# Normalising the tokens of a latent stage on ScalarE by scale and shift instead of on VectorE by mean and scale

## The chip, the core and the metric

The kernel runs on one core of one Trainium2 chip. The metric is the device time of one execution in microseconds, the median of three timed runs. Beside it stands one profiled execution, whose trace is read here. A core has five engines that run their own queues in order and wait for each other by semaphores: TensorE (PE; its weight loads are PEld), VectorE (DVE), ScalarE (ACT), GpSimd (POOL), and SyncE (SP), which here only issues DMAs.

## What is computed

Two layers of attention and experts over 4096 tokens of 256 numbers. The change touches the first step alone, the normalisation of the first layer's input, whose result goes to the attention and to the experts. The reference, cut to that:

```python
def _layernorm(x, axis=-1, eps=1e-05):
    m = jnp.mean(x, axis=axis, keepdims=True)
    v = jnp.var(x, axis=axis, keepdims=True)
    return (x - m) / jnp.sqrt(v + eps)

x = L0_attn_x                       # (2, 2048, 256)
xn = _layernorm(x, axis=-1)
x = x + _L0_attn_ref(xn, ...) + _L0_ffn_ref(xn, ...)

# first lines of _L0_attn_ref(xn, ...)
q = (x @ Wqa @ Wqb).reshape(b, s, H, D)
kv = (x @ Wkva @ Wkvb).reshape(b, s, KVH, D, 2)
k, v = (kv[..., 0], kv[..., 1])
q = _rope(q)
k = _rope(k)
```

## The kernel before

The program is a row of stages with a barrier between each two: `latents`, `attention`, `layer1_weights`, `experts`, `mixing`, `layer1`, `finish`. The change is in `latents`, which makes the normalised tokens, the queries, keys and values of the first layer and the router's logits.

`latents` cuts the 4096 tokens into 8 chunks (c = 0 to 7) of 512, each of four tiles (t) of 128 tokens. A chunk goes through these steps:

- VectorE: `statistics` (`bn_stats` over each tile, L397), `variances` (`bn_aggr`, then `var_eps`, the variance plus epsilon, four numbers per partition, L402 to L406). ScalarE: `std`, a square root (L278). VectorE: `normalise` (reciprocal `rstd`, L410, then (x - mean) * rstd for each of four tiles of 128x256, L415) into `xn`.
- TensorE: `turn` transposes the chunk (L347) into `pT`; ScalarE copies it to `xnT` (L283). TensorE: `combined` makes the latents (L355), ScalarE copies them to `comb` (L287).
- TensorE: three `pair`s (k = 0, 1, 2) of products (L363): queries in two halves, keys in the third. VectorE: `products` multiplies each pair by cosine and sine (`by_cos` L424, `by_sin` L425).
- Each of the three is then split into three bf16 parts. GpSimd: `turned` adds the two products to `rot` (L252). ScalarE: `high` (L292). GpSimd: `left` subtracts to `rest` (L258). ScalarE: `mid` (L296). VectorE: `low` (L429). SP stores the parts.
- TensorE and VectorE: values and logits (L369, L372, L435, L437).

Nothing but the order in which the code is written sets the order on an engine. A chunk c on VectorE does products 0, `statistics(c+2)`, products 1, products 2, `variances(c+2)`, low 0, `values`, `normalise(c+2)`, low 1, low 2. On ScalarE: the two copies to `xnT` of chunk c+1, high 0, mid 0, high 1, the copy to `comb` of chunk c+1, high 2, `std_of(c+2)`, mid 1, mid 2. On GpSimd: rot 0, rest 0, rot 1, rot 2, rest 1, rest 2. On TensorE: pair 0, `turn(c+1)`, pair 1, pair 2, `combined(c+1)`, values and logits. The first two chunks are normalised ahead of the loop. Chunks 6 and 7 have nothing left to normalise.

Of the kernel before, what the change touches and what calls it, by code (L numbers as in the profile page):

```python
# [24 lines left out]
ALU = mybir.AluOpType  # L25
ACT = mybir.ActivationFunctionType
# [75 lines left out]
def latents(nc, d, s):  # L102

    with ExitStack() as ctx:  # L104
        def sb(name, shape, dt=F32):
            return ctx.enter_context(nc.sbuf_tensor(name, shape, dt))
# [21 lines left out]
        mean_var = sb("mean_var", [P, TPC, 2])  # L128
        var_eps = sb("var_eps", [P, TPC])
        std = sb("std", [P, TPC])  # L130
        rstd = sb("rstd", [P, TPC])
        xn = [sb(f"xn{u}", [P, TPC, E]) for u in range(2)]
        xnT = [sb(f"xnT{u}", [P, EC, CH]) for u in range(2)]
        comb = [sb(f"comb{u}", [COMB, CH]) for u in range(2)]
# [140 lines left out]
        def _(act):  # L275
            def std_of(c):
                act.wait_ge(var_ready, 5 * c + 5)
                act.activation(std[:], var_eps[:], ACT.Sqrt).then_inc(std_ready, 1)  # L278

            def xnT_copy(c):  # L280
                act.wait_ge(xnT_made, c + 1)
                for k in range(EC):
                    act.copy(xnT[c % 2][:, k], pT[:, k]).then_inc(xnT_ready, 1)  # L283
# [14 lines left out]
            def chunk(c):  # L298
                if c + 1 < NCH:
                    xnT_copy(c + 1)  # L300
                high(c, 0)
                mid(c, 0)
                high(c, 1)
                if c + 1 < NCH:
                    comb_copy(c + 1)
                high(c, 2)
                if c + 2 < NCH:
                    std_of(c + 2)
                mid(c, 1)
                mid(c, 2)  # L310

            for dst, src in (
# [5 lines left out]
            ):  # L318
                act.dma_start(dst, src).then_inc(weights_in, 16)
            std_of(0)  # L320
            act.wait_ge(weights_in, 16 * 5)

            q_pair = wqb[0:QL].rearrange("k (n two) -> k n two", two=2)
# [3 lines left out]
            for dst, src in (  # L327
# [3 lines left out]
            ):  # L331
                act.copy(dst, src).then_inc(swapped, 1)
            std_of(1)
            xnT_copy(0)
            comb_copy(0)
            for c in range(NCH):
# [56 lines left out]
        def _(dve):  # L393
# [4 lines left out]

            def variances(c):
                dve.wait_ge(stats_ready, 4 * c + 4)  # L400
                wait(dve, xn_ready, 4 * c)
                dve.memset(carrier[:], 0.0)  # L402
                for t in range(TPC):
                    dve.bn_aggr(mean_var[:, t], stats[:, t]).then_inc(var_ready, 1)
                dve.wait_ge(var_ready, 5 * c + 4)
                dve.tensor_scalar(var_eps[:], mean_var[:, :, 1], LN_EPS, None, ALU.add).then_inc(var_ready, 1)  # L406

            def normalise(c):
                dve.wait_ge(std_ready, c + 1)
                dve.reciprocal(rstd[:], std[:]).then_inc(rstd_ready, 1)  # L410
                dve.wait_ge(rstd_ready, c + 1)
                wait(dve, xn_out[c % 2], 16 * (c // 2))
                wait(dve, xnT_made, c - 1)
                for t in range(TPC):
                    dve.tensor_scalar(xn[c % 2][:, t], x[c % 2][:, t], mean_var[:, t, 0:1], rstd[:, t:t + 1],  # L415
                                      ALU.subtract, ALU.mult).then_inc(xn_ready, 1)

            def products(c, k):
                n = PAIRS * c + k
# [19 lines left out]
            def chunk(c):  # L439
                ahead = c + 2 < NCH  # L440
                products(c, 0)
                if ahead:
                    statistics(c + 2)
                products(c, 1)
                products(c, 2)
                if ahead:
                    variances(c + 2)
                low(c, 0)
                values(c)
                if ahead:  # L450
                    normalise(c + 2)
                low(c, 1)
                low(c, 2)

# [6 lines left out]
            for c in range(2):  # L461
                statistics(c)
                variances(c)
                normalise(c)
            dve.wait_ge(tables_in, 32)
            for c in range(NCH):
                chunk(c)
# [2060 lines left out]
```

## Time and profile before

| | us |
|---|---|
| median of three runs | 2151.51 |
| lowest, highest | 2150.54, 2153.01 |
| the profiled execution, its own time | 2145.62 |
| span of its trace | 2143.9 |

Over the span TensorE is busy 92%, VectorE 72%, ScalarE 48%, GpSimd 23%. `latents` ends at 120.4 us, and 62.6 of GpSimd's 492.4 us lie in it. Times in the rows below count from the span's start. A timeline row gives the start, the busy time, the engine, line, operation, what it writes and reads with its shape, and how many instructions it merges ("x2"); in brackets stands how long the engine had been idle and who released it.

### The profile page before, as it was taken

To read this page: it belongs to the slowest core of one execution; us is meant where nothing else is said; L and a number is where in the kernel's file an instruction comes from. 1 tells how busy PE (TensorE), PEld (TensorE's weight loads), DVE (VectorE), ACT (ScalarE), POOL (GpSimd) and SP (SyncE) were. 2 spreads that over 40 slices of the span, in tenths; PEclk is the share of its full clock that TensorE was granted. 3 is DMA by queue.
4 is the path that set the end of the run, shared out by engine and by line. 5 is a ranking of instruction groups with operands and counts; after the bars stand their busy time and mean duration, and the time that the engine had idled before them with its cause. 6 is when DMAs were issued, how large, how long until landed. Compare 5 with 4: busy or idle time off the path is not lost. (4 is left out here: it accounts for less than half of the span.)

```text
span 2143.9 us, 35036 instructions
## 1 busy us (share of the span) xinstructions
PE 1973.5 (92%) x11857; PEld 1190.7 (56%) x11874; DVE 1549.3 (72%) x3492; ACT 1026.7 (48%) x2224; POOL 492.4 (23%) x908
## 2 busy tenths in 40 slices
PE   7869999999999999999579999996878999999998
PEld 3313333333333333332279999995656777777777
DVE  6879888888888888885145333324669998899893
ACT  3406677777777777777444444543331122221112
POOL 4621133322222222222223333335600000000000
PEclk9958999999999999999889999998889999999998
DMA  5572011111111111100332322214510000000005
GB/s 189 186 230 78 29 46 58 56 43 41 41 43 43 42 43 41 43 21 11 92 114 88 110 97 88 89 45 148 167 55 2 18 20 20 20 20 20 3 11 169
DMA packets 119460, 143.69 MB, mean 67 GB/s; under 512 B 12152, under 2 KB 107008, under 8 KB 118912
## 3 DMA queue, kind: packets, MB, share of 16 engines
q1 hardware_dynamic: 89392, 99.48, 14.5%
q0 software_dynamic: 7680, 20.98, 3.1%
q10 hardware_dynamic: 22224, 21.16, 2.9%
q8 instruction: 88, 1.44, 0.3%
q14 instruction: 76, 0.62, 0.1%
HBM read 85.10 MB, written 56.10 MB: 66 GB/s over the span
## 5 line engine op out<-in xcount | busy, mean ns | idle before, releaser
L715 ACT ACTIVATE at_wt<-at_B 128x512 f32<-128x512 f32 (+3 forms) x1280 | 606.9, 538 | 243.0 <-PE at_B L764 237.1
L965 DVE TENSOR_REDUCE at_piece_max<-at_A 128x1 f32<-128x512 f32 x768 | 487.1, 683 | 53.0 <-PE at_A L745 51.1
L782 PE MATMUL at_O<-at_wt,at_v 128*32 128x512 f32 (+3 forms) x2560 | 312.3, 540 | 0.0
L669 POOL TENSOR_SCALAR_AFFINE_SELECT at_wt<-at_wt 128x128 f32<-128x128 f32 x512 | 147.8, 294 | 658.9 <-ACT at_wt L715 650.2
L745 PE MATMUL at_A<-at_k,at_q 96*128 96x512 bf16 (+3 forms) x800 | 275.2, 353 | 8.5 <-DVE at_piece_max L962 2.4
L962 DVE CUSTOM_DVE_ANT_0 at_junk<-at_A,at_hide 128x128 bf16<-128x128 f32 (+3 forms) x512 | 230.3, 487 | 65.9 <-PE at_A L745 62.9
L764 PE MATMUL at_B<-at_q,at_k 99*128 99x512 bf16 (+3 forms) x800 | 272.7, 348 | 2.0 <-ACT at_wt L715 2.0
L1425 PE MATMUL ex_H<-ex_xT,ex_w_in 128*128 128x256 f32 x1920 | 247.4, 285 | 3.2 <-DVE ex_xT L1532 3.2
L1425 PEld LDWEIGHTS ex_H<-ex_xT,ex_w_in 128*128 128x128 f32 x1920 | 236.5, 192 | 3.6 <-DVE ex_w_out L1537 3.6
L1546 DVE TENSOR_TENSOR ex_h<-ex_act_a,ex_H 128x256 f32<-128x256 f32 x160 | 66.8, 417 | 212.4 <-ACT ex_act_a L1474 212.3
L745 PEld LDWEIGHTS at_A<-at_k,at_q 96*128 96x128 bf16 x800 | 77.7, 97 | 214.7 <-DVE at_piece_max L965 108.9
L745 PE MATMUL at_A<-s_k,s_q 96*128 96x512 bf16 (+2 forms) x480 | 175.8, 384 | 20.9 <-PEq L104 9.6
L2111 ACT ACTIVATE l_act_g<-l_G 128x512 f32<-128x512 f32 x80 | 47.9, 599 | 305.2 <-PE l_G L2025 249.9
L1467 POOL TENSOR_TENSOR ex_hT<-ex_h,ex_hT 128x256 fp32r<-128x256 f32 x160 | 123.2, 774 | 265.5 <-ACT ex_hT L1478 265.5
L764 PE MATMUL at_B<-s_q,s_k 99*128 99x512 bf16 x480 | 160.2, 352 | 4.7 <-ACT at_wt L715 4.1
L2046 PE MATMUL l_D<-s_down,l_h 128*128 128x256 f32 x640 | 153.6, 383 | 3.5 <-DVE l_h L2192 3.5
L2046 PEld LDWEIGHTS l_D<-s_down,l_h 128*128 128x128 f32 x640 | 120.1, 191 | 35.0 <-issue 13.5
L2166 DVE TENSOR_TENSOR l_order<-l_order 128x1024 f32<-128x1024 f32 x112 | 136.9, 1222 | 1.9
L2020 PE MATMUL l_G<-l_xp,s_gate_up 128*128 128x512 f32 x480 | 137.2, 420 | 0.0
L2164 DVE TENSOR_TENSOR l_order<-l_order 128x1024 f32<-128x1024 f32 x112 | 136.5, 1219 | 0.0
L745 PEld LDWEIGHTS at_A<-s_k,s_q 96*128 96x128 bf16 x480 | 47.0, 99 | 151.1 <-DVE at_piece_max L965 76.8
L2030 PE MATMUL l_U<-l_xp,s_gate_up 128*128 128x512 f32 x480 | 130.2, 406 | 0.0
(262 smaller groups left out, 2633.3 us busy)
## 6 DMA issues: line engine op xcount, KB each, us to landing
buf<-s_down ACTq DMA_DIRECT2D x10, 1024.0 KB, 10.5
ex_x<-buf SPq DMA_DIRECT2D x40, 256.0 KB, 2.7
expert_out<-ex_y ACTq DMA_DIRECT2D x40, 256.0 KB, 2.2
ex_raw_in<-in_W_in SPq DMA_DIRECT2D x8, 1024.0 KB, 4.9
q_parts<-parts SPq DMA_DIRECT2D x16, 384.0 KB, 3.4
s_down<-in_x SPq DMA_DIRECT2D x8, 512.0 KB, 4.8
xn<-xn SPq DMA_DIRECT2D x8, 512.0 KB, 5.6
at_v<-v SPq DMA_DIRECT2D x16, 256.0 KB, 3.4
```

Source lines behind the costliest of these rows:

```text
L669: pool.affine_select(block_, block_, [[1, P]], ALU.is_ge, 0.0, base=0, channel_multiplier=-1).then_inc(hidden, 1)
L715: act.activation(wt[(HP * p + h) % NE_][:, q0:CH], pB_of(p, h, u)[:, q0:CH], ACT.Exp, scale=D ** -0.5).then_inc(wt_ready, 1)
L745: pe.matmul(pA[slot % NA][:, 0:w], q[n % 3][0:STACK, h, i * P:(i + 1) * P], k[n % 3][0:STACK, k0:k0 + w], start=True, stop=True).then_inc( ...
L764: pe.matmul(pB_of(p, h, u)[:, q0:CH], k[n % 3][:, kt * P:(kt + 1) * P], q[n % 3][:, h, j * CH + q0:(j + 1) * CH], start=True, stop=True).t ...
L782: pe.matmul(pO[j % 2][rows, q0:CH], vs[n % 3][:, kt // TPC, kt % TPC, :], wt[(HP * p + h) % NE_][:, q0:CH], start=kt < 2 and not late, sto ...
L962: ins = dve.tensor_tensor_reduce(junk[(HP * i + h) % 4][:, 0:w], pA[slot % NA][:, 0:w], hide[:, CH - w:CH], 1.0, NEG, ALU.add, ALU.max, ac ...
L965: ins = dve.tensor_reduce(top, pA[slot % NA][:, 0:w], AX.X, ALU.max)
L1425: ins = pe.matmul(pH[f][:, a, :], w_in[w][wq][:, k, cols], xT[i][xq][:, k, :], start=(n == 0), stop=(n == len(terms) - 1))
L2020: ins = pe.matmul(pG[i % 2][:], s[f"gate_up{b}"][:, e, k, :], xp[c % 2][:, a, k, :], start=(a, b, k) == steps[0], stop=(e >= NX and (a, b, ...
L2046: ins = pe.matmul(pD[t // 2][:, t % 2, :], h[i % 2][:, t * P:(t + 1) * P], s["down"][:, ORDER[i], :], start=False, stop=(i == MLPS - 1 and ...
L2164: dve.tensor_tensor(dv[:, :, half:size], high, low_m, ALU.min).then_inc(sort_step, 1)
L2166: dve.tensor_tensor(dv[:, :, 0:half], low, high_m, ALU.max).then_inc(sort_step, 1)
```

## The change

The four normalisations of a chunk move from VectorE to ScalarE. There xn = rstd * x + shift is one activation per tile, with scale and bias read per partition. VectorE makes rstd and shift = -mean * rstd (`scales`, one reciprocal and one `scalar_tensor_tensor` on four numbers per partition) in two buffers each. `variances(c+2)` goes ahead of products 2, and `scales(c+2)` stands right behind products 2. On ScalarE `std_of(c+2)` goes ahead of the copy to `comb`, and the four activations (`normal(c+2)`) stand between mid 1 and mid 2. For the first two chunks, `normal(0)` stands behind the first `std`, and `normal(1)` behind the second, ahead of the first copy to `xnT`.

```diff
--- before.py
+++ after.py
@@ -128,7 +128,8 @@
         mean_var = sb("mean_var", [P, TPC, 2])
         var_eps = sb("var_eps", [P, TPC])
         std = sb("std", [P, TPC])
-        rstd = sb("rstd", [P, TPC])
+        rstd = [sb(f"rstd{u}", [P, TPC]) for u in range(2)]
+        shift = [sb(f"shift{u}", [P, TPC]) for u in range(2)]
         xn = [sb(f"xn{u}", [P, TPC, E]) for u in range(2)]
         xnT = [sb(f"xnT{u}", [P, EC, CH]) for u in range(2)]
         comb = [sb(f"comb{u}", [COMB, CH]) for u in range(2)]
@@ -277,6 +278,14 @@
                 act.wait_ge(var_ready, 5 * c + 5)
                 act.activation(std[:], var_eps[:], ACT.Sqrt).then_inc(std_ready, 1)
 
+            def normal(c):
+                act.wait_ge(rstd_ready, 2 * c + 2)
+                wait(act, xn_out[c % 2], 16 * (c // 2))
+                wait(act, xnT_made, c - 1)
+                for t in range(TPC):
+                    act.activation(xn[c % 2][:, t], x[c % 2][:, t], ACT.Identity, bias=shift[c % 2][:, t:t + 1],
+                                   scale=rstd[c % 2][:, t:t + 1]).then_inc(xn_ready, 1)
+
             def xnT_copy(c):
                 act.wait_ge(xnT_made, c + 1)
                 for k in range(EC):
@@ -301,12 +310,14 @@
                 high(c, 0)
                 mid(c, 0)
                 high(c, 1)
+                if c + 2 < NCH:
+                    std_of(c + 2)
                 if c + 1 < NCH:
                     comb_copy(c + 1)
                 high(c, 2)
+                mid(c, 1)
                 if c + 2 < NCH:
-                    std_of(c + 2)
-                mid(c, 1)
+                    normal(c + 2)
                 mid(c, 2)
 
             for dst, src in (
@@ -318,6 +329,7 @@
             ):
                 act.dma_start(dst, src).then_inc(weights_in, 16)
             std_of(0)
+            normal(0)
             act.wait_ge(weights_in, 16 * 5)
 
             q_pair = wqb[0:QL].rearrange("k (n two) -> k n two", two=2)
@@ -331,6 +343,7 @@
             ):
                 act.copy(dst, src).then_inc(swapped, 1)
             std_of(1)
+            normal(1)
             xnT_copy(0)
             comb_copy(0)
             for c in range(NCH):
@@ -398,22 +411,20 @@
 
             def variances(c):
                 dve.wait_ge(stats_ready, 4 * c + 4)
-                wait(dve, xn_ready, 4 * c)
+                wait(dve, rstd_ready, 2 * c)
                 dve.memset(carrier[:], 0.0)
                 for t in range(TPC):
                     dve.bn_aggr(mean_var[:, t], stats[:, t]).then_inc(var_ready, 1)
                 dve.wait_ge(var_ready, 5 * c + 4)
                 dve.tensor_scalar(var_eps[:], mean_var[:, :, 1], LN_EPS, None, ALU.add).then_inc(var_ready, 1)
 
-            def normalise(c):
+            def scales(c):
                 dve.wait_ge(std_ready, c + 1)
-                dve.reciprocal(rstd[:], std[:]).then_inc(rstd_ready, 1)
-                dve.wait_ge(rstd_ready, c + 1)
-                wait(dve, xn_out[c % 2], 16 * (c // 2))
-                wait(dve, xnT_made, c - 1)
-                for t in range(TPC):
-                    dve.tensor_scalar(xn[c % 2][:, t], x[c % 2][:, t], mean_var[:, t, 0:1], rstd[:, t:t + 1],
-                                      ALU.subtract, ALU.mult).then_inc(xn_ready, 1)
+                wait(dve, xn_ready, 4 * (c - 1))
+                dve.reciprocal(rstd[c % 2][:], std[:]).then_inc(rstd_ready, 1)
+                dve.wait_ge(rstd_ready, 2 * c + 1)
+                dve.scalar_tensor_tensor(shift[c % 2][:], mean_var[:, :, 0], -1.0, rstd[c % 2][:],
+                                         ALU.mult, ALU.mult).then_inc(rstd_ready, 1)
 
             def products(c, k):
                 n = PAIRS * c + k
@@ -442,13 +453,13 @@
                 if ahead:
                     statistics(c + 2)
                 products(c, 1)
+                if ahead:
+                    variances(c + 2)
                 products(c, 2)
                 if ahead:
-                    variances(c + 2)
+                    scales(c + 2)
                 low(c, 0)
                 values(c)
-                if ahead:
-                    normalise(c + 2)
                 low(c, 1)
                 low(c, 2)
 
@@ -461,7 +472,7 @@
             for c in range(2):
                 statistics(c)
                 variances(c)
-                normalise(c)
+                scales(c)
             dve.wait_ge(tables_in, 32)
             for c in range(NCH):
                 chunk(c)
```

One chunk on ScalarE, from its copies to `xnT` to the next ones, before:

```order
L283 COPY xnT<-pT 128x512 x2
L292 CAST parts<-rot 128x512
L296 CAST parts<-rest 128x512
L292 CAST parts<-rot 128x512
L287 COPY comb<-pC 104x512
L292 CAST parts<-rot 64x512
L278 ACTIVATE std<-var_eps 128x4
L296 CAST parts<-rest 128x512
L296 CAST parts<-rest 64x512
L283 COPY xnT<-pT 128x512 x2
```

and changed:

```order
L292 COPY xnT<-pT 128x512 x2
L301 CAST parts<-rot 128x512
L305 CAST parts<-rest 128x512
L301 CAST parts<-rot 128x512
L279 ACTIVATE std<-var_eps 128x4
L296 COPY comb<-pC 104x512
L301 CAST parts<-rot 64x512
L305 CAST parts<-rest 128x512
L286 ACTIVATE xn<-s_down,shift,rstd 128x256 x4
L305 CAST parts<-rest 64x512
```

The square root stands two places earlier, and four activations stand between the last two `mid` (parts<-rest). No table load stands in either.

The same chunk on VectorE, from its second products to its first `low` and the values, before:

```order
L424 TENSOR_TENSOR by_cos<-pR,cos 128x512 [waits lat_pair_made]
L425 TENSOR_TENSOR by_sin<-pR,sin 128x512
L424 TENSOR_TENSOR by_cos<-pR,cos 64x512 [waits lat_pair_made]
L425 TENSOR_TENSOR by_sin<-pR,sin 64x512
L402 MEMSET carrier 128x1 [waits lat_xn_ready,lat_stats_ready]
L404 BN_AGGR mean_var<-stats 128x2 x4
L406 TENSOR_SCALAR var_eps<-mean_var 128x4 [waits lat_var_ready]
L429 TENSOR_TENSOR parts<-rest,parts 128x512 [waits lat_mid_ready]
```

and changed:

```order
L435 TENSOR_TENSOR by_cos<-pR,cos 128x512 [waits lat_pair_made]
L436 TENSOR_TENSOR by_sin<-pR,sin 128x512
L415 MEMSET carrier 128x1 [waits lat_rstd_ready,lat_stats_ready]
L417 BN_AGGR mean_var<-stats 128x2 x4
L419 TENSOR_SCALAR var_eps<-mean_var 128x4 [waits lat_var_ready]
L435 TENSOR_TENSOR by_cos<-pR,cos 64x512 [waits lat_pair_made]
L436 TENSOR_TENSOR by_sin<-pR,sin 64x512
L424 RECIPROCAL rstd<-std 128x4 [waits lat_xn_ready,lat_std_ready]
L426 SCALAR_TENSOR_TENSOR shift<-mean_var,rstd 128x4 [waits lat_rstd_ready]
L440 TENSOR_TENSOR parts<-rest,parts 128x512 [waits lat_mid_ready]
```

The aggregates and `var_eps` stand ahead of the third products instead of behind them, and reciprocal and shift ahead of the first `low` instead of behind the values.

Ahead of the loop, the changed ScalarE, from the copies of weights to the first copy of turned tokens:

```order
L344 COPY wv<-wkvb 32x64
L279 ACTIVATE std<-var_eps 128x4 [waits lat_var_ready]
L286 ACTIVATE xn<-s_down,shift,rstd 128x256 [waits lat_rstd_ready]
L286 ACTIVATE xn<-s_down,shift,rstd 128x256 x3
L292 COPY xnT<-pT 128x512 [waits lat_xnT_made]
```

Before, the copy to `xnT` stood right behind the square root.

## Rows read from the trace of the kernel before

**Rows 1.** Windows, first stage: length; busy us of PE, PEld, DVE, ACT, POOL; clock; DMA

```profile
0.00:120.40 120.40, 85.83 (x288) 40.38 (x288) 87.38 (x212) 45.93 (x87) 62.64 (x61) 0.95 0.55 182
```

**Rows 2.** Windows, each from one chunk's first `by_cos` to the next one's; columns as above

```profile
21.58:33.94 12.36, 10.77 (x45) 5.73 (x44) 11.42 (x26) 5.46 (x10) 7.65 (x6) 1.00 0.18 54
33.94:45.88 11.94, 9.74 (x38) 4.62 (x37) 10.48 (x28) 5.38 (x10) 7.61 (x6) 1.00 0.60 194
45.88:58.51 12.63, 11.30 (x38) 4.99 (x37) 11.14 (x27) 5.47 (x10) 7.75 (x6) 0.86 0.53 181
...
70.46:83.33 12.87, 11.35 (x40) 5.45 (x39) 11.34 (x28) 5.47 (x10) 7.62 (x6) 0.89 0.56 184
83.33:95.27 11.94, 9.73 (x38) 4.62 (x37) 10.48 (x27) 5.37 (x10) 7.62 (x6) 1.00 0.55 188
95.27:106.20 10.93, 10.38 (x33) 4.31 (x31) 7.05 (x12) 5.27 (x9) 7.56 (x6) 1.00 0.55 191
```

**Rows 3.** Timeline of chunk 5

```profile
86.43 0.67 DVE L425 TENSOR_TENSOR by_sin<-pR,sin 128x512 f32<-128x512 f32 x1
86.67 1.16 POOL L258 TENSOR_TENSOR rest<-rot,parts 128x512 f32<-128x512 f32 x1 [0.73 <-ACT parts L292]
...
87.79 3.01 POOL L252 TENSOR_TENSOR rot<-by_cos,by_sin 128x512 f32<-128x512 f32 x2
...
88.63 0.46 DVE L406 TENSOR_SCALAR var_eps<-mean_var 128x4 f32<-128x4 f32 x1
...
90.76 2.26 POOL L258 TENSOR_TENSOR rest<-rot,parts 128x512 f32<-128x512 f32 x2
...
91.81 1.37 DVE L415 TENSOR_SCALAR xn<-s_down,mean_var,rstd 128x256 f32<-128x256 f32 x1
91.95 0.62 ACT L296 CAST parts<-rest 128x512 bf16<-128x512 f32 x1 [0.39 <-POOL rest L258]
93.06 0.62 ACT L296 CAST parts<-rest 64x512 bf16<-64x512 f32 x1 [0.49 <-POOL rest L258]
94.07 1.28 DVE L429 TENSOR_TENSOR parts<-rest,parts 128x512 bf16<-128x512 f32 x2
...
94.20 1.09 PE L347 MATMUL pT<-s_ident,xn 128*128 128x128 f32 x8 [1.97 <-DVE xn L415]
```

**Rows 4.** Timeline of chunk 0 (first row) and chunk 4

```profile
27.95 2.15 DVE L406 TENSOR_SCALAR var_eps<-mean_var 128x4 f32<-128x4 f32 x1
...
75.29 1.26 POOL L252 TENSOR_TENSOR rot<-by_cos,by_sin 128x512 f32<-128x512 f32 x1 [0.34 <-DVE by_sin L425]
...
75.79 0.68 DVE L424 TENSOR_TENSOR by_cos<-pR,cos 64x512 f32<-64x512 f32 x1 [0.57 <-PE pR L363]
...
77.00 0.17 DVE L404 BATCH_NORM_AGGREGATE mean_var<-stats 128x2 f32<-128x6 f32 x1
...
77.40 1.07 DVE L406 TENSOR_SCALAR var_eps<-mean_var 128x4 f32<-128x4 f32 x1
```

**Rows 5.** Timeline of the start, ahead of the loop

```profile
10.69 0.52 ACT L332 COPY wqb_swap<-wqb 64x128 f32<-64x128 f32 x2 [2.88 <-DMA wkvb<-in_Wkvb]
...
11.93 0.20 ACT L278 ACTIVATE std<-var_eps 128x4 f32<-128x4 f32 x1
12.04 1.05 ACT L283 COPY xnT<-pT 128x512 f32<-128x512 f32 x2
...
12.38 1.38 DVE L415 TENSOR_SCALAR xn<-s_down,mean_var,rstd 128x256 f32<-128x256 f32 x4
...
21.58 0.69 DVE L424 TENSOR_TENSOR by_cos<-pR,cos 128x512 f32<-128x512 f32 x1 [7.82 <-PE pR L363]
```

**Rows 6.** ScalarE in later stages: group (count, busy us, mean ns, idle), then timeline rows

```profile
L1732 ACT ACTIVATE mx_xn<-mx_x,mx_shift,mx_rstd 128x256 f32<-128x256 f32 x32 | 17.5, 593 | 8.0 <-DVE mx_shift L1792 8.0
...
1560.65 1.09 ACT L1732 ACTIVATE mx_xn<-mx_x,mx_shift,mx_rstd 128x256 f32<-128x256 f32 x2 [0.50 <-DVE mx_shift L1792]
...
1595.96 1.71 ACT L2127 ACTIVATE s_down<-s_down,l_mean 128x256 f32<-128x256 f32 x4 [4.61 <-DVE l_mean L2258]
```

## What I expected

> **What bounds the kernel now.** I read the windows by stage first. The first stage (`latents`) takes 120.4 us of the 2143.9 us span [rows 1], and the change touches nothing else. What follows starts behind a barrier and keeps its instructions, so a microsecond won or lost in `latents` is a microsecond of the kernel. Then I cut the stage at the start of each chunk's first product (`by_cos`). That gives the period of each chunk: 12.36, 11.94, 12.63, 11.95, 12.87, 11.94 us for chunks 0 to 5, and 10.93 for chunk 6 [rows 2]. Chunks 0 to 5 each normalise chunk c+2; chunk 6 doesn't. So at most the normalising costs 73.69 - 6 x 10.93 = 8.1 us in all. Of the six, chunks 1, 3 and 5 repeat each other to 0.01 us; chunks 0, 2 and 4 are longer.
>
> Last I read the timeline of chunk 5 backwards from 95.27, where the next chunk's first product starts [rows 3]. VectorE has no gap there: two `low` (1.28 us from 94.07), before them the four normalisations from 91.81. The first of them alone lasts 1.37 us, until just behind GpSimd's last `rest` (90.76 + 2.26 = 93.02); where GpSimd is idle, all four take 1.38 [rows 5]. ScalarE had its last `mid` done at 93.06 + 0.62 = 93.68, so the second `low`, which starts about 0.6 us after the first, at 94.67, waits for VectorE alone. TensorE waits for the same four: its turning of the tokens starts at 94.20 after 1.97 us idle. So two chains run side by side between GpSimd and the next product: the four normalisations on VectorE, done at 94.1, and mid(c,2) on ScalarE, done at 93.7 with its low a microsecond later. Under both lies GpSimd's own loop (rot, rest, rot, rot, rest, rest), the 10.93 us of chunk 6.
>
> **The change, part by part.**
>
> *Price of the moved step.* The same operation with scale and bias read per partition, 128x256, stands in the mixing stage: 593 ns each, and two in a row take 1.09 us, so the next starts 0.50 us after the one before [rows 6]. Four take 3 x 0.50 + 0.59 = 2.09 us, and the next ScalarE instruction starts 2.0 us after the first. With a scale alone four took 1.71 us [rows 6]; that is my lower bound. On VectorE they were 1.38 (alone) to 2.34 us. A page speaks against such a move: the Trainium skill, "ScalarE: Activation LUTs", section "Rules for kernel authors", says to keep multiplying and adding on VectorE. It gives no sum here, and the rows (2.09 against 1.38) lean its way. No table load is added: the sequence of ScalarE shows none.
>
> *Where it stands.* ScalarE does mid(c,1), then the four, then mid(c,2). In chunk 5, mid(c,1) runs 91.95 to 92.57 and rest(c,2) is ready at 93.02 [rows 3]. Only 0.5 us of the 2.0 lies in a gap of ScalarE. mid(c,2) would start at 92.5 + 2.0 = 94.5 instead of 93.06, end at 95.15, and low(c,2) start at 95.2 instead of 94.67: **+0.5 us**. The next product follows low(c,2) as before. low(c,1), now free of the four, is done before and helps nobody. TensorE gets its tokens at about 94.6 instead of 94.15 and stays as late as the product is. The break-even of the four is 1.5 us.
>
> *What is pushed ahead of the third products.* `variances` now stands between products(c,1) and products(c,2). In chunk 5 the second products end at 86.43 + 0.67 = 87.10. The aggregates take 0.40 us (77.00 to 77.40 in [rows 4]), so `var_eps` is issued at 87.5, inside GpSimd's rest(c,0), which runs to 87.83. The rows show that `var_eps`, four numbers per partition, waits for GpSimd: 88.63 + 0.46 = 89.09, just behind the end of rot(c,1) [rows 3]. In chunk 0 it lasted 2.15 us, through the end of one GpSimd instruction and a whole further one [rows 4]. So it ends at about 87.9, the third products at 89.2, and rot(c,2) starts at 89.25 instead of 89.05: +0.2. Before, low(c,0) stepped between rot(c,1) and rot(c,2), and the two took 3.01 us instead of 2 x 1.26 [rows 3]. Now it comes later, behind `scales`, and steps in behind rot(c,2) or behind rest(c,1). In the first case rest(c,1) ends some 0.35 us later than before, in the second at about the same time. Of these two cases I take **+0.1**, between 0 and 0.35. A page bears on them: the Trainium skill, "SBUF — State Buffer", section "Who interferes with whom", says that a VectorE operation with two SBUF inputs and a GpSimd one that reads SBUF exclude each other for the length of an instruction. By that rule `shift`, which has two, waits for rot(c,2) and lets rest(c,1) go ahead of low(c,0), the second case, and the sum would be 0.3 us less; no row here shows a `shift` beside GpSimd.
>
> With the +0.5 above that makes +0.6 us a chunk for chunks 1, 3 and 5, bounds +0.2 (four at 1.71 us) and +0.9.
>
> *Chunks 0, 2 and 4.* There TensorE is late with the second pair. In chunk 4 its granted clock averages 0.89 [rows 2]. rot(c,1) starts at 75.29, right behind products(c,1), and runs to 76.55 [rows 4]. `var_eps` comes 0.4 us behind the products, at 75.6, so inside rot(c,1), and waits for its end. Before, products(c,2) started at 75.79; now they start at 76.65: **+0.85** for rot(c,2), rest(c,1) and mid(c,1). Walked on: products to 77.95, rot(c,2) 78.03 to 79.29, a short `shift`, rest(c,1) to 80.6, mid(c,1) to 81.2, the four to 83.2, mid(c,2) to 83.75, low(c,2) to 84.5, next product at 84.4 instead of 83.33: +1.1. I walked chunks 0 and 2 the same way and got +1.2 and +1.15. If low(c,0) steps in ahead of rest(c,1) it is +1.45. I take **+1.15** each, bounds +0.7 and +1.5.
>
> *Hidden.* `std` now goes ahead of the copy of comb: that delays the copy by 0.2 us, and TensorE's next products, which need comb, stand just ahead of its 1.97 us of waiting [rows 3]. The reciprocal and `shift` end by 90.8 in chunk 5 even if `shift` waits for rot(c,2); the four start at 92.5. The order of SP's queue is unchanged; low(c,0) and its store come 1.6 us later, and nobody reads that store for a chunk and more.
>
> *Start.* This part is bare. xnT_copy(0) stood right behind std(1), at 12.04 [rows 5]. Now normal(1) stands between. It needs the reciprocal and `shift` behind std(1). In the mixing stage, where reciprocal and shift stand between them in the same way, ScalarE sits idle 0.50 us [rows 6]; std(1) ends at 12.13, so the four start at 12.6. 12.6 + 2.0 = 14.6 for xnT_copy(0): **+2.55 us**. VectorE's first product waited 7.82 us for TensorE at 21.58 [rows 5], and TensorE for this copy, so nothing covers it. normal(0) starts half a microsecond behind the first `std`, at 8.3, and ends near 10.4, ahead of the weights, which ScalarE takes up at 10.69 [rows 5]; it costs nothing. Bounds: +2.2 (four at 1.71) and +3.4, if TensorE's rise to the higher of its clocks falls later in its own work too (0.85, as chunks with time at the lower clock are 0.7 to 0.9 us longer [rows 2]).
>
> *Sum.* 2.55 + 3 x 0.6 + 3 x 1.15 = 7.8 us. The profiled execution took 2145.62 us; the three timed ones have the median 2151.51, 5.9 more, and I add the difference to that: **2159.3 us** (+0.36%). By the bounds: 2.2 + 0.6 + 2.1 = 4.9 and 3.4 + 2.7 + 4.5 = 10.6.
>
> **The rivals.**
>
> *A, no change.* The loop is more elastic than my walk: GpSimd's three last instructions are no longer disturbed by VectorE, `var_eps` slips between two of them in all chunks, and the four cost about 1.7 us. Then a chunk pays 0.2 us: 2.2 + 6 x 0.2 = +3.4, 2154.9 us. For it: GpSimd's pairs take 3.01 where two undisturbed ones take 2 x 1.26 [rows 3, 4]. Against: `var_eps` was held in each chunk whose rows stand here (0.46, 1.07 and 2.15 us, where four numbers alone want under 0.2).
>
> *B, faster.* The four vanish beside ScalarE's waits, and each chunk falls to GpSimd's 10.93 us. That is -8.1 + 2.55 = -5.5 us, 2146.0. Place: between mid(c,1) and mid(c,2). It decides from a length of the four of 0.5 us, the gap there; the rows give 2.0. For it speaks only that ScalarE is busy 5.4 of 12 us [rows 2].
>
> *C, slower still.* `var_eps` loses to rot(c,1) in chunks 1, 3 and 5 too, as it lost one more GpSimd instruction in chunk 0 [rows 4]. Each then pays 1.2 us more: +3.6, in all +11.4, 2162.9. On the same side: TensorE, idle longer in each chunk, is granted the lower of its two clocks (1.2 and 2.4 GHz) more often. It had it, after its wait for the tokens, in chunks 2 and 4, and those were 0.7 and 0.9 us longer than chunk 5 [rows 2].
>
> Beyond the stage one thing is not fixed: attention begins at the lower clock, and the end of that stretch may move by a microsecond either way.
>
> **How the numbers follow.** Forecast (+4.3 to +10 us) 0.62, A 0.19, B 0.04, C 0.15. A measurement of this kernel tells 0.2%, 4.3 us, from no change. A lies within it, B beyond it on the fast side. So faster 0.04, same 0.19, slower 0.77. The range leaves out B, the half of A near zero and the tail of C: 2154.0 to 2164.0.
>
> **What would show it.** The four activations at 0.50 us spacing, mid(c,2) starting right behind them, with low(c,2) waiting for it on VectorE; chunk periods near 12.5 and 13.5 to 14, chunk 6 still 10.9; `var_eps` ending just behind a GpSimd instruction; first product at 24.1. I am wrong if the four are much shorter, if mid(c,2) still waits for rest(c,2), or if the period of chunks 1, 3, 5 stays at 11.9. Then the start alone is left and the kernel is unchanged within the measurement.

## The result and the profile after

The changed kernel takes 2162.06 us in the median of six runs (2157.49 to 2162.6), against 2150.43 us for the kernel before in six runs (2146.95 to 2153.01). The ratio is 1.005, with a 95% interval of 1.0038 to 1.0063: 0.5% slower. Measured once more, in experiment e10, the ratio is 1.006 (1.0039 to 1.0082). I had forecast 2159.3 us and a range of 2154 to 2164.

The profiled execution took 2161.9 us, its span is 2160.2. Attention's first matmul starts at 129.91 us, where it started at 120.44 before. So 9.5 us of the difference between the two traces lie in `latents`. The rest, 6.8 us, lies in stages whose instructions are the same in both: from attention's first matmul to the next stage's 942.6 us against 939.3, and 516.5 against 513.3 in `layer1`. The two later traces, e10 of the changed kernel and e11 of the kernel before, show nearly the same again: 941.9 against 939.7, and 516.4 against 513.4. The longer `layer1` is not the change's, since two versions of the kernel before, e5 and e8, have it too (516.4 and 516.5). What lengthens attention by 2 to 3 us stays open.

One timed run of e3 took 2801.02 us at a mean granted clock of 0.647, and e3's ratio is without it.

The stage, cut at each chunk's first `by_cos` as in [rows 2] (length; busy us of PE, PEld, DVE, ACT, POOL with counts; granted clock; DMA share; GB/s):

```profile
23.93:36.14 12.21, 10.74 (x45) 5.70 (x44) 10.29 (x24) 7.34 (x14) 7.67 (x6) 1.00 0.19 54
36.14:48.07 11.93, 9.72 (x37) 4.61 (x37) 10.07 (x24) 7.23 (x14) 7.65 (x6) 1.00 0.60 193
48.07:61.84 13.77, 11.32 (x37) 5.02 (x37) 10.35 (x25) 7.34 (x14) 7.70 (x6) 0.88 0.52 169
61.84:75.71 13.87, 11.31 (x37) 5.01 (x37) 10.34 (x25) 7.34 (x14) 7.69 (x6) 0.87 0.48 166
75.71:89.75 14.04, 11.35 (x37) 5.05 (x36) 10.34 (x24) 7.34 (x14) 7.69 (x6) 0.86 0.50 168
89.75:103.79 14.04, 11.35 (x36) 5.43 (x36) 10.35 (x24) 7.34 (x14) 7.70 (x6) 0.86 0.52 168
103.79:115.61 11.82, 11.82 (x36) 5.41 (x34) 6.55 (x12) 5.37 (x9) 7.55 (x6) 0.90 0.52 171
```

Chunks 0 and 1 are as long as before (12.21 and 11.93 against 12.36 and 11.94). Chunks 2 to 5 are longer by 1.14, 1.92, 1.17 and 2.10 us, and chunk 6 by 0.89. From chunk 2 on TensorE has the lower of its two clocks for a part of every chunk (a mean granted clock of 0.86 to 0.90). Before, that was so in chunks 2 and 4 (0.86 and 0.89), and for a moment in chunk 3 (0.98). ScalarE is busy 7.3 us of a chunk, where it was 5.4.

The timeline of chunk 4 (start, busy time, what, idle before and releaser), which answers to [rows 4] and to the end of [rows 3]:

```profile
79.16 0.69 DVE L435 TENSOR_TENSOR by_cos<-pR,cos 128x512 f32<-128x512 f32 x1 [0.86 <-PE pR L376]
...
80.52 1.27 POOL L253 TENSOR_TENSOR rot<-by_cos,by_sin 128x512 f32<-128x512 f32 x1 [0.32 <-DVE by_sin L436]
80.78 1.04 DVE L419 TENSOR_SCALAR var_eps<-mean_var 128x4 f32<-128x4 f32 x1
...
83.08 1.26 POOL L253 TENSOR_TENSOR rot<-by_cos,by_sin 64x512 f32<-64x512 f32 x1 [1.29 <-DVE by_sin L436]
83.12 1.24 DVE L426 SCALAR_TENSOR_TENSOR shift<-mean_var,rstd 128x4 f32<-128x4 f32 x1
...
84.28 0.68 DVE L440 TENSOR_TENSOR parts<-rest,parts 128x512 bf16<-128x512 f32 x1
84.30 2.78 POOL L259 TENSOR_TENSOR rest<-rot,parts 128x512 f32<-128x512 f32 x2
...
86.53 2.07 ACT L286 ACTIVATE xn<-s_down,shift,rstd 128x256 f32<-128x256 f32 x4
...
88.51 0.60 ACT L305 CAST parts<-rest 64x512 bf16<-64x512 f32 x1
...
88.65 1.51 PE L360 MATMUL pT<-s_ident,xn 128*128 128x128 f32 x8 [2.69 <-ACT xn L286]
...
89.14 0.68 DVE L440 TENSOR_TENSOR parts<-rest,parts 64x512 bf16<-64x512 f32 x1 [1.50 <-ACT parts L305]
```

Read it from the top. TensorE is late with the second pair. rot(c,1) starts behind it, and `var_eps`, issued 0.26 us later, is held until rot(c,1) ends. The third products wait for `var_eps`, so GpSimd sits idle 1.29 us ahead of rot(c,2). Then the four activations take 2.07 us, mid(c,2) starts right behind them, and low(c,2) waits for mid(c,2). TensorE waits 2.69 us for the tokens, where no such wait was above 1.97 us in the kernel before (the one of chunk 5 stands in [rows 3]). The lower clock begins during the eight transposes behind the wait: they take 1.51 us here, 1.09 at the higher clock.

`shift` is issued 0.04 us behind the start of rot(c,2) and held until that ends, 1.24 us. Then low(c,0) starts 0.02 us ahead of rest(c,1), and the two `rest` take 2.78 us, where they took 2.26 in [rows 3]. So it is in chunks 2 to 5. In chunks 0 and 1 `shift` is held by rest(c,1) as well, for 1.70 and 1.45 us, and low(c,0) comes behind rest(c,1).

The start, which answers to [rows 5]:

```profile
11.77 0.21 ACT L279 ACTIVATE std<-var_eps 128x4 f32<-128x4 f32 x1
...
12.42 2.07 ACT L286 ACTIVATE xn<-s_down,shift,rstd 128x256 f32<-128x256 f32 x4 [0.44 <-DVE shift L426]
14.40 1.04 ACT L292 COPY xnT<-pT 128x512 f32<-128x512 f32 x2
...
23.93 0.69 DVE L435 TENSOR_TENSOR by_cos<-pR,cos 128x512 f32<-128x512 f32 x1 [11.54 <-PE pR L376]
```

The copy starts at 14.40 instead of 12.04, 2.36 us later, and the first product at 23.93 instead of 21.58, 2.35 us later.

### The profile page after: what moved, and what is told of

It is laid out like the page before. It is cut to its first block and busy times, and to the rows that moved or that the text cites. A ratio compares the mean times of both kernels' runs of the same rounds, so it can differ in the third digit from the quotient of the medians.

```text
span 2160.2 us, 35067 instructions
## 1 busy us (share of the span) xinstructions
PE 1986.9 (92%) x11874; PEld 1197.5 (55%) x11874; DVE 1543.2 (71%) x3468; ACT 1042.5 (48%) x2256; POOL 492.4 (23%) x908
## 5 line engine op out<-in xcount | busy, mean ns | idle before, releaser
L2057 PEld LDWEIGHTS l_D<-s_down,l_h 128*128 128x128 f32 x640 | 120.5, 191 | 33.0 <-issue 13.5
```

What stands on the lines that cost most here:

```text
L2057: ins = pe.matmul(pD[t // 2][:, t % 2, :], h[i % 2][:, t * P:(t + 1) * P], s["down"][:, ORDER[i], :], start=False, stop=(i == MLPS - 1 and ...
```

## The experiments

Two theories stood against each other behind the result. Theory 1 is the layout of the queues: the block of activations and `var_eps` under rot(c,1) make a chunk long by themselves. Theory 2 is the clock: the longer wait for the tokens brings the lower clock in each chunk, and that makes the second pair late. "Attention" below is the start of its first matmul; it tells the length of the stage free of what happens in later ones. It has in it the start of the first product, which moves by some 1.8 us between traces without any edit (last section), so the table at the end also gives the time from the first product to attention. e1 to e4 ran on a chip on which the kernel before is 1.5% slower (2182.18 us); every ratio is to the kernel before on the same chip.

**e4: TensorE kept busy in its wait.** In the changed kernel, in front of the turning:

```diff
             def turn(c):
-                pe.wait_ge(xn_ready, 4 * c + 4)
                 wait(pe, xnT_ready, 2 * c)
                 wait(pe, vl_ready, 2 * (c - 1))
+                if c > 1:
+                    for _ in range(16):
+                        pe.transpose(pT[:, 0, 0:P], ident[:], ident[:])
+                pe.wait_ge(xn_ready, 4 * c + 4)
```

> The changed kernel with 16 extra transposes of the identity into pT on TensorE ahead of each turn from chunk 2 on, in the time in which it waits for the tokens (2.7 us idle; 16 take 2.2 us at the higher clock). Theory 2 (the lower clock, granted once in each of chunks 2 to 5 behind the long wait, makes the second pair late and so puts var_eps under rot(c,1)): no half-clock stretch inside the chunks, periods of chunks 2 to 5 at 11.9 to 12.5 us instead of 13.8 to 14.0, attention's first matmul at about 123 us, the kernel 5 to 7 us faster than the changed one. Theory 1: the periods stay above 13.3 us.

Measured: attention at 122.95 us, 7.0 earlier than in the changed kernel; ratio to before 1.0023 (1.0006 to 1.004), against 1.005 (1.0038 to 1.0063) without the filler. Windows by chunk:

```profile
23.91:37.71 13.80, 12.86 (x61) 7.88 (x60) 10.36 (x23) 7.35 (x14) 7.72 (x6) 1.00 0.18 48
37.71:49.66 11.95, 11.21 (x52) 6.12 (x52) 10.09 (x24) 7.23 (x14) 7.67 (x6) 1.00 0.61 194
49.66:61.62 11.96, 11.46 (x55) 6.37 (x53) 10.09 (x25) 7.24 (x14) 7.67 (x6) 1.00 0.62 192
...
85.53:97.58 12.05, 11.45 (x55) 6.36 (x53) 10.29 (x25) 7.24 (x14) 7.66 (x6) 1.00 0.56 186
```

TensorE does more work, and chunks 2 to 5 are 1.8 to 2.1 us shorter, chunk 6 0.9: Theory 2. With the higher clock throughout, a chunk with the four activations on ScalarE takes 11.95 us (chunk 5 12.05), against 11.94 before the change. The block as such costs next to nothing there.

The exception is chunk 0, 13.80 us, which is a case of theory 1 in the same trace. Here the second pair is 0.35 us late for another reason (TensorE reaches its full speed later than in the changed kernel's trace: the transposes at 23.6 us take 1.76 us, 1.40 there), and `var_eps` falls under rot(0,1):

```profile
28.48 1.27 POOL L253 TENSOR_TENSOR rot<-by_cos,by_sin 128x512 f32<-128x512 f32 x1
28.73 1.04 DVE L422 TENSOR_SCALAR var_eps<-mean_var 128x4 f32<-128x4 f32 x1
```

In the changed kernel's chunk 0 it came just ahead of rot(0,1) and was not held:

```profile
28.39 0.17 DVE L419 TENSOR_SCALAR var_eps<-mean_var 128x4 f32<-128x4 f32 x1
28.41 1.27 POOL L253 TENSOR_TENSOR rot<-by_cos,by_sin 128x512 f32<-128x512 f32 x1
```

That chunk took 12.21 us. The filler is not the reason, since chunk 0 of e1 has none, has `var_eps` held 1.06 us, and takes 13.70. So a `var_eps` that falls on the wrong side of rot(c,1) goes with 1.6 us at the same granted clock. Both theories are right in part: the lower clock makes the second pair late, and the late pair puts `var_eps` under rot(c,1).

**e5: the same filler (12 transposes) in the kernel before.**

```diff
+                if c > 1:
+                    for _ in range(12):
+                        pe.transpose(pT[:, 0, 0:P], ident[:], ident[:])
                 pe.wait_ge(xn_ready, 4 * c + 4)
```

> The kernel before with 12 extra transposes of the identity into pT on TensorE ahead of each turn from chunk 2 on, in its 2.0 us of waiting. If the clock alone makes chunks 2 and 4 of the kernel before long, all of chunks 1 to 5 take 11.94 us, no half-clock stretch falls into them, and attention starts about 1.6 us earlier than 120.4, at 118.8 (less what chunk 0 does, which no filler reaches). Then the change and the kernel before, both with filler, differ by the start alone: 2.4 us against the 122.95 that the changed kernel with filler showed. Rival: the filler delays the tokens' turning or leaves the periods as they are.

Measured: chunks 1 to 5 at 11.96 to 11.97 us with a granted clock of 1.00, attention at 119.05, ratio 0.9985 (0.9972 to 0.9998). So chunks 2 and 4 of the kernel before, 12.63 and 12.87, were long through the clock. The two kernels with filler differ by 3.9 us at attention's start, not by the 2.4 expected: 2.38 us are between the first products (23.91 against 21.53), and 1.28 in chunk 0 (13.80 against 12.52). The other chunks are equal within 0.1 us.

**e2: variances back behind the third products**, std and scales back with them; the activations stay between the two mid.

```diff
                 products(c, 1)
-                if ahead:
-                    variances(c + 2)
                 products(c, 2)
                 if ahead:
-                    scales(c + 2)
+                    variances(c + 2)
                 low(c, 0)
                 values(c)
+                if ahead:
+                    scales(c + 2)
```

> The changed kernel, but variances(c+2) stands behind the third products again, std behind high(c,2), and scales where the normalisation stood, behind the values. The four activations stay between the last two mid on ScalarE. Theory 1 (var_eps held by rot(c,1) ahead of the third products makes the chunks of 13.8 to 14.0 us): they fall to 12.4 to 12.8 us, the block of activations alone costs about 0.5 to 0.8 us a chunk, and the kernel is about 3 to 5 us faster than the changed one. Theory 2 (the lower clock in each chunk makes them long): the periods stay at 13.5 to 14 as long as TensorE waits as long for its tokens.

Measured: attention at 128.30, ratio 1.0048 (1.0027 to 1.0069). The last two chunks with activations:

```profile
75.46:88.82 13.36, 11.34 (x39) 5.74 (x38) 9.70 (x24) 7.34 (x14) 7.73 (x6) 0.88 0.52 177
88.82:102.19 13.37, 11.36 (x40) 5.52 (x39) 9.70 (x25) 7.34 (x14) 7.71 (x6) 0.88 0.54 174
```

Chunks 0 to 3 took 13.02, 14.65, 12.37 and 13.17 us. Neither theory's number came. In the last two chunks, the new place of variances, `std` and scales costs 0.7 us of 14.04, and the other 1.4 us above 11.95 are there without it. Over the stage nothing is won: from the first product to attention it takes 106.05 us, the changed kernel 105.98. TensorE's waits were 2.0 to 2.6 us.

**e3: the move of variances and std alone, in the kernel before.**

```diff
                 products(c, 1)
-                products(c, 2)
                 if ahead:
                     variances(c + 2)
+                products(c, 2)
                 low(c, 0)
                 values(c)
                 if ahead:
                     normalise(c + 2)
```

> The kernel before, with only variances(c+2) moved ahead of the third products and std ahead of the copy to comb; the reciprocal and the normalisation stay on VectorE where they were. Theory 1: where TensorE is late with the second pair, the third products start 0.9 us later and the chunk is longer by up to 0.9 us; the other chunks by 0.2. In all 2 to 3.5 us slower than before. Theory 2: no more half-clock stretches than before (2), so within 1 us of before.

Measured: ratio 0.9998 (0.9981 to 1.0014), attention at 116.44, 4.0 us *earlier* than before. Chunks 1 and 5:

```profile
33.08:44.71 11.63, 9.72 (x38) 4.61 (x37) 11.16 (x27) 5.36 (x10) 7.57 (x6) 1.00 0.58 199
...
79.64:91.27 11.63, 9.73 (x38) 4.61 (x37) 11.16 (x27) 5.36 (x10) 7.58 (x6) 1.00 0.56 187
```

I had expected a loss by Theory 1 and no difference by Theory 2. In chunk 5 the reciprocal starts 7.15 us behind the chunk's start instead of 8.26. The four normalisations then take longer, 3.15 us instead of 2.34, but end 0.3 us earlier in the chunk, and the wait for the tokens falls from 1.97 to 1.56 us. In this trace no chunk had the lower clock. The timed runs are too scattered to show those few microseconds.

**e1: chunks 0 and 1 normalised on VectorE in the changed kernel**, the rest as changed.

```diff
             std_of(0)
-            normal(0)
...
             std_of(1)
-            normal(1)
```

> The changed kernel, but chunks 0 and 1 are normalised on VectorE as before. In the changed kernel the first product starts at 23.93 us of the span and attention's first matmul at 129.9, against 21.58 and 120.4 before. If the start is a bare term of the sum, both move back by 2.4 us (21.6 and 127.5) and the time falls by 2.4 us. Rival: the chunks behind it are bound by themselves and by how the clock falls on them, and the first chunks only shift; then the first product moves and attention's start does so by another amount, since the half-clock stretches meet the chunks elsewhere.

Measured: the first product at 21.50 us, 2.4 earlier, as expected. But attention at 129.07, only 0.8 earlier, and ratio 1.0047 (1.0029 to 1.0064). Chunk 0 took 13.70 us (`var_eps` held 1.06 us, as in e4) and chunk 5 14.91, at a granted clock of 0.83; chunk 6 kept the higher clock and took 10.93. The rival's case came. The start is bare, but most of what it gives back was lost again in this trace. A term of the stage's start does not simply add while the later chunks can take the one form or the other. The end of chunk 0 has a wait that the lower clock did not follow: chunk 1 took 11.95 us.

```profile
34.10 1.09 PE L358 MATMUL pT<-s_ident,xn 128*128 128x128 f32 x8 [2.71 <-ACT xn L286]
```

**e6: the activations behind mid(c,2).**

```diff
                 mid(c, 1)
+                mid(c, 2)
                 if c + 2 < NCH:
                     normal(c + 2)
-                mid(c, 2)
```

> The changed kernel with the four activations behind mid(c,2) instead of ahead of it. Theory 1 (the block between the two mid is what the next product waits for): low(c,2) and the next chunk's first product come earlier, the period falls. Theory 2 (what counts is how long TensorE waits for its tokens): mid(c,2) is early but the tokens come 0.6 us later still, TensorE's wait grows to above 3 us, the lower clock stays in each chunk and the second pair comes later by the same amount: periods stay at 13.5 us or more.

Measured: ratio 1.0092 (1.007 to 1.0114), attention at 141.39. Chunks 3 and 4, and TensorE's wait between them:

```profile
64.44:80.46 16.02, 12.22 (x36) 5.89 (x36) 10.34 (x24) 7.35 (x15) 7.70 (x6) 0.79 0.42 143
80.46:96.48 16.02, 12.69 (x36) 6.02 (x36) 10.34 (x24) 7.35 (x15) 7.70 (x6) 0.79 0.43 144
```

```profile
81.85 1.97 PE L360 MATMUL pT<-s_ident,xn 128*128 128x128 f32 x8 [3.80 <-ACT xn L286]
```

low(c,2) no longer waits for the block, and the chunk is about 2 us longer than in the changed kernel. When TensorE gets its tokens counts for more than when low(c,2) is done.

**e7: two tiles on each engine.** From chunk 2 on, tiles 0 and 1 on VectorE behind the values, tiles 2 and 3 on ScalarE.

```diff
-                for t in range(TPC):
+                for t in range(0 if c < 2 else 2, TPC):
                     act.activation(xn[c % 2][:, t], x[c % 2][:, t], ACT.Identity, ...
...
                 low(c, 0)
                 values(c)
+                if ahead:
+                    normal_half(c + 2)      # dve.tensor_scalar on tiles 0 and 1
```

> The changed kernel with two of the four tiles of each chunk from 2 on normalised on VectorE, behind the values, and two on ScalarE between the two mid. The block on ScalarE is 1.0 us instead of 2.0. TensorE's wait falls under 2 us if VectorE is not held by GpSimd. Theory 2: fewer half-clock stretches than in the changed kernel, periods between 11.6 and 12.5 us, attention's first matmul near 122 to 124. Theory 1 gives about the same periods but with the half-clock stretches left.

Measured: every chunk from 1 to 5 at 11.40 us, attention at 115.80, both below what I had expected; ratio 0.9986 (0.997 to 1.0002).

```profile
79.16:90.56 11.40, 9.73 (x38) 4.62 (x37) 10.53 (x27) 6.36 (x12) 7.65 (x6) 1.00 0.60 189
90.56:101.48 10.92, 10.37 (x33) 4.30 (x31) 7.05 (x12) 5.27 (x9) 7.55 (x6) 1.00 0.63 207
```

```profile
78.09 1.09 PE L360 MATMUL pT<-s_ident,xn 128*128 128x128 f32 x8 [1.34 <-DVE xn L436]
```

**e9: the split of e7, and chunks 0 and 1 on VectorE** by the edit of e1.

> Two of four tiles on VectorE and two on ScalarE from chunk 2 on, and chunks 0 and 1 on VectorE alone. If the start is a term of its own, the periods stay at the 11.40 us of the split and attention's first matmul comes 2.4 us earlier than 115.8 where the clock rises alike: 113 to 114 us. The kernel is then 5 to 7 us faster than before (ratio 0.997). If the start is no bare term, 115 us or more and a ratio of 0.998 or above.

Measured: the same 11.40 us, attention at 113.42, ratio 0.9987 (0.9971 to 1.0003). Attention starts 7.0 and 5.0 us earlier than in the two traces of the kernel before (120.44 and 118.46); the second has its first product at 19.80 us, as e9 has at 19.75, so 5.0 is the like for like. The time is lower by 0.13%, which the measurement does not tell from no change. It is the best version I have; I can't call it faster.

**e8: all four on VectorE, right behind the third products**, with variances and std moved as in e3.

```diff
                 products(c, 1)
+                if ahead:
+                    variances(c + 2)
                 products(c, 2)
                 if ahead:
-                    variances(c + 2)
+                    normalise(c + 2)
                 low(c, 0)
                 values(c)
-                if ahead:
-                    normalise(c + 2)
```

> The kernel before with variances ahead of the third products, std ahead of the copy to comb, and the normalisation still on VectorE, but right behind the third products, ahead of low(c,0). If what costs is how late the tokens are, TensorE no longer waits for them, no half-clock stretch falls into the stage, and the periods fall below the 11.64 us that moving variances alone gave, toward the 10.93 of chunk 6: attention's first matmul at 113 to 116 us against 120.4, 4 to 7 us faster than before. Rival: the four normalisations, held by GpSimd's instructions in the middle of the chunk, delay the copies of the values and low(c,0), and the period stays at 11.6 or more.

Measured: ratio 1.0027 (1.0013 to 1.004), attention at 124.96, though the first product came at 19.52. In the middle of the chunk rot(c,2) and the two `rest` of GpSimd run one behind the other, and the four, which take 1.38 us where GpSimd is idle, take 4.01. They push the copy of the logits back, for which TensorE then waits:

```profile
78.95 4.01 DVE L415 TENSOR_SCALAR xn<-s_down,mean_var,rstd 128x256 f32<-128x256 f32 x4
...
84.14 1.47 PE L347 MATMUL pT<-s_ident,xn 128*128 128x128 f32 x8 [2.34 <-DVE s_logits L437]
```

The rival of that expectation holds: 13.67 us a chunk. The lower clock is there in each chunk from 2 on.

**e10 and e11: both kernels once more.**

> The changed kernel once more. If the lower clock in chunks 2 to 5 follows from the length of TensorE's wait and not from chance, this profile shows it again: three or four half-clock stretches inside the chunks, periods of 13.5 to 14 us there. If it was chance, one or two stretches and periods near 12 in the others. The ratio to before should be 1.003 to 1.006.

> The kernel before once more, for its trace. If the two half-clock stretches in it are typical, the periods are again 11.94 us with one to three chunks of 12.4 to 12.9; if they depend on chance, there can be none or many.

Measured: the changed kernel repeats itself to 0.2 us a chunk (12.13, 11.94, 13.86, 14.05, 14.02, 14.04, 11.69; attention at 129.99; ratio 1.006). The lower clock is there in chunk 6 too, so in five chunks where I had expected three or four. The four long chunks come back, so they are not chance. The kernel before has another pattern: of chunks 1 to 5 chunk 3 alone is long (12.87), chunk 6 takes 11.82, attention is at 118.46; ratio to the other runs of the same kernel 0.9998 (0.9981 to 1.0015). Where its lower clock falls changes from trace to trace, and behind each such stretch inside the chunks the next wait is a short one (1.33 to 1.52 us).

Put side by side, with the wait of TensorE just ahead of its turning, in chunks behind the first:

| kernel | wait, us | chunks 1 to 6 with a granted clock under 0.95 | usual chunk, us | first product to attention, us |
|---|---|---|---|---|
| e7, e9 (split) | 1.3 | none | 11.40 | 93.7, 93.7 |
| e3 | 1.6 | none | 11.64 | 95.2 |
| before (two traces) | 1.3 to 2.0 | 2, 2 | 11.94, long ones 12.6 to 12.9 | 98.9, 98.7 |
| changed (two traces) | 1.8, then 2.5 to 2.7 | 5, 5 | 13.8 to 14.0 | 106.0, 106.0 |
| e1 | 1.9, then 2.7, last 2.2 | 4 | 13.8 to 14.9 | 107.6 |
| e2 | 2.0 to 2.4 | 6 | 12.4 to 14.7 | 106.1 |
| e8 | 2.3 | 5 | 13.67 | 105.4 |
| e6 | 3.3 to 3.8 | 6 | 15.0 to 16.0 | 119.1 |
| e4, e5 (wait filled) | filled | none | 11.95 | 99.0, 97.5 |

Counted over the turnings of all traces without filler, chunk 0's among them: behind the 25 waits of up to 1.6 us the granted clock never fell. It fell behind 10 of the 15 waits of 1.84 to 2.02 us, and behind 24 of the 26 of 2.2 us and more. The two exceptions are both in e1 (2.71 and 2.22 us). So a longer wait goes with the lower clock more often, but the wait alone does not settle it.

## Why the prediction was right, point by point

**What bounds the stage.** Right in the view of VectorE and ScalarE behind GpSimd. But I had TensorE stay "as late as the product is", with no cost of its own. e6 shows that it has one: freeing the product and delaying the tokens by the same block makes the chunk 2 us longer.

**Price of the four.** I took 2.09 us from the mixing stage; they took 2.07 in every chunk. They stand between the two mid, mid(c,2) follows at once, low(c,2) waits for it: all as walked.

**Chunks 1, 3, 5: +0.6.** Mis-sized, for a chunk at the higher clock: 11.93 to 11.96 us in the changed kernel and in e4, against 11.94: 0.0 (chunk 5 of e4, 12.05, is +0.1). The +0.5 rested on mid(c,1) ending where it did before, 9.24 us behind the chunk's start (92.57 - 83.33). In the changed kernel's chunk 1 low(c,0) no longer takes its turn between rot(c,1) and rot(c,2), and the block starts earlier:

```profile
42.87 1.45 DVE L426 SCALAR_TENSOR_TENSOR shift<-mean_var,rstd 128x4 f32<-128x4 f32 x1
...
44.85 2.07 ACT L286 ACTIVATE xn<-s_down,shift,rstd 128x256 f32<-128x256 f32 x4
46.83 0.60 ACT L305 CAST parts<-rest 64x512 bf16<-64x512 f32 x1
```

44.85 is 8.71 us behind the chunk's start at 36.14; I had put it at 9.2. So the half microsecond was there before I began to add. I had the order of low(c,0) as a matter of +0.1, and it was about -0.5.

**Chunks 0, 2, 4: +1.15.** The first half of the mechanism is the one of the trace: `var_eps` issued inside rot(c,1) and held 1.04 us, the third products behind it. The second half is not: I walked a short `shift` with rest(c,1) ahead of low(c,0), and in chunks 2 to 5 low(c,0) stepped in ahead, the case for which I had put +1.45. The size still held for chunks 2 and 4 (+1.14, +1.17), in chunk 4 partly because rot(c,2) started 7.37 us behind the chunk's start and not at the 7.57 of my walk. That the two errors cancel is luck. The size failed for chunk 0 (-0.15), where `var_eps` slipped in 0.02 us ahead of rot(0,1).

`shift` was held by GpSimd: 1240 ns in the median and up to 1696, against 161 where GpSimd is idle. By the rule of the Trainium skill ("SBUF — State Buffer", "Who interferes with whom") that I had cited, two SBUF inputs are enough for that, and the trace agrees. The order that I had drawn from it, rest(c,1) ahead of low(c,0), came in chunks 0 and 1 and not in 2 to 5.

**Number of such chunks.** This is the step that failed most. I took three, 0, 2 and 4, as in the trace of before. There were four, 2 to 5, and chunks 3 and 5 paid 1.92 and 2.10 us, beyond my bound of +0.9. Chunk 6, for which I had nothing, paid 0.89. I had named the reason, TensorE idle longer and so more often at the lower clock, as a side remark to rival C, and given it no number. The traces of both kernels suggest why it stays. In the kernel before, a chunk with the lower clock is followed by a shorter wait (1.33 us ahead of chunk 3), and the clock stays up. In the changed one the held `var_eps` pushes the tokens back too, the next wait is 2.45 us, and the lower clock comes again. That the clock is in the cause is shown by e4, where filling the wait took 7.0 us off the stage. That `var_eps` closes the loop is argued from the traces and not shown: e2 took it out of its place and still had a granted clock of 0.83 to 0.94 in every chunk from 0 to 6, at waits of 2.0 to 2.6 us.

**Start: +2.55.** Measured 2.35: ScalarE idled 0.44 instead of 0.50, and `std` came 0.16 us earlier. As a term of the kernel's time it is less sure, as e1 showed. In e10 and e11 the first products are 4.16 us apart (23.96 against 19.80), some 1.8 of it because TensorE reached its full speed earlier in e11.

**Sum.** I had 2.55 + 1.8 + 3.45 = 7.8. The traces give 2.35 + 6.17 for chunks 0 to 5 + 0.89 for chunk 6 = 9.4 in the stage, and the timed runs 10.7 by the ratio (8.2 to 13.5), at the edge of my bounds of 4.9 to 10.6. Errors of opposite sign kept the total inside the range. I had +1.75 for chunks 0 and 1 together, which paid -0.16; I had +1.2 for chunks 3 and 5 together and nothing for chunk 6, which paid 4.9. So the slowdown and its place in the chunk were foreseen, and that the time came out near is in part luck.

**Rivals.** A (no change) wanted blocks of 1.7 us and an elastic `var_eps`; B (faster) wanted the block to vanish. Both fell, but with the higher clock kept up (e4, chunks 1 to 5) the whole block does nearly vanish against the 11.94 us of before, and with half of it (e7, e9) a chunk takes 11.40, still above the 10.93 of B. C's first mechanism, `var_eps` held in chunks 3 and 5, did occur, by way of its second, the clock; chunk 1 was spared. C's 2162.9 us lies nearer to the measured 2162.06 than my 2159.3 does.

## What to carry to other kernels

When a step moves to another engine, ask how long the matmul engine waits for its result, not only when the next instruction in the chain starts. A wait that grew from 1.97 to 2.45 us and more cost two microseconds a round here, as the lower clock followed in each. Compare a candidate by the start of the next stage as well as by the median, and look whether a slow round is followed by a shorter or a longer wait. And before moving four of four, try two of four: here the two engines then worked side by side and the wait was the shortest of all, though the kernel's time did not fall by more than the measurement can tell.

## What the runs showed of the hardware

Extra work on TensorE made the stage shorter: 16 idle transposes a chunk, at a granted clock of 1.00, took a chunk from 14.0 to 11.95 us. A VectorE operation on four numbers per partition can cost over a microsecond: `var_eps` took 0.17 us alone and 1.04 when issued 0.26 us behind the start of a GpSimd addition, and whether it came 0.02 us before or 0.25 us behind that start went with 1.6 us of the chunk. The moment at which TensorE reaches its full speed at the start of the program also moves: with the same instructions up to there, the first product came at 23.93 us in the changed kernel and at 22.14 in e7, where the first pair ran at twice the speed. The granted clock of the windows does not show it: it reads 1.00 in both traces there, and only the durations tell:

```profile
20.06 2.05 PE L376 MATMUL pR<-comb,wqb 104*128 104x512 f32 x2 [0.77 <-ACT comb L296]
```

```profile
20.08 1.10 PE L376 MATMUL pR<-comb,wqb 104*128 104x512 f32 x2 [0.77 <-ACT comb L296]
```

The first line is the changed kernel, the second e7. One and the same kernel has both forms too: the first product of the kernel before came at 21.58 us in one trace and at 19.80 in the other (e11). So the stage's start carries an uncertainty of nearly 2 us that no edit made.
